# A vision-tower layer on one core: the attention weighing in fp16 parts from the second batch on, one exp for two heads, and relu's high half cast by GpSimd

## What is computed

```python
h = einsum('bhid,oi,od->bho', x, weighted_sum, weight)            # x: (8, 512, 256, 4) -> h: (8, 512, 256)
t = layernorm(h)
q, k, v = split(t @ qkv_w.T + qkv_b)                               # 16 heads of 16
q, k = unit(rotate(q)), unit(rotate(k))                            # rotary, then divided by the norm
attn = softmax(einsum('bhqd,bhkd->bhqk', q, k) * 16 ** -0.5)
h = h + einsum('bhqk,bhkd->bhqd', attn, v) @ out_w.T + out_b
y = layernorm(h)
w = sigmoid(y @ Wg + bg); w = w * (w > 0.5)                        # gates of 8 experts
h = h + sum_e w[:, e] * (relu(y @ W1[e] + b1[e]) @ W2[e] + b2[e])  # 256 -> 1024 -> 256
```

## Time and profile before

| What | us |
|---|---|
| median of 3 runs | 2003.24 |
| the profiled execution | 2003.1 |
| its span, first to last instruction | 2001.2 |
| busy TensorE matmuls in it | 1898.5 (95%) |
| busy ScalarE | 1143.7 (57%) |
| busy VectorE | 780.0 (39%) |
| busy GpSimd | 675.3 (34%) |

### The profile page before, as it was taken

One profiled execution on the slowest core, in us unless ns is written; L12 is line 12 of the kernel. 1 busy time (PEld: TensorE's weight loads), 2 busy tenths in 40 slices (PEclk: granted clock), 3 DMA queues, 4 the chain that ended last, 5 costly groups with the idle time before them and its releaser, 6 DMA issues.

```text
span 2001.2 us, 33188 instructions
## 1 busy us (share of the span) xinstructions
PE 1898.5 (95%) x13120; PEld 1207.9 (60%) x13120; DVE 780.0 (39%) x1664; ACT 1143.7 (57%) x1969; POOL 675.3 (34%) x570
## 2 busy tenths in 40 slices
PE   5679898899999999999999999999999999999999
PEld 4237543567546764577646775467645776466666
DVE  5756943547213480045602472134800456022000
ACT  2654576544765457644765547654576447655444
POOL 1103422324323353333423343233533334234443
PEclk8679999899999999999999999999999999999999
DMA  4013342242212221132212322122211322113221
GB/s 156 25 60 106 106 147 85 96 168 69 80 64 106 95 85 64 64 121 80 85 64 85 116 69 80 64 106 95 85 64 64 121 81 85 64 64 116 105 86 54
DMA packets 40475, 176.67 MB, mean 88 GB/s; under 512 B 4072, under 2 KB 17152, under 8 KB 23936
## 3 DMA queue, kind: packets, MB, share of 16 engines
q1 hardware_dynamic: 40320, 174.54, 24.9%
HBM read 153.55 MB, written 20.97 MB: 87 GB/s over the span
## 4 chain that ended last, share of the span: by engine, by line
PE 78%; DVE 8%; issue 6%; ACT 2%; POOL 1%; POOLq 0%; DVEq 0%; ACTq 0%
PE bank_h L859 29%; PE bank_f L878 10%; PE bank_f L880 10%; PE bank_f L881 10%; PE bank_o L787 5%; PE bank_s L775 3%; PE bank_s L691 3%; PE bank_s L692 2%; PE bank_s L693 2%; PE bank_s L760 1%; DVE qk L981 1%; DVE tmp_b L976 1%; DVE y L899 1%; POOL hl L547 1%; PE bank_s L827 1%
## 5 line engine op out<-in xcount | busy, mean ns | idle before, releaser
L547 POOL TENSOR_TENSOR hl<-h,hh 128x512 f16<-128x512 f32 x512 | 607.5, 1187 | 1125.5 <-ACT hh L668 693.3
L859 PE MATMUL bank_h<-x,w1s 128*128 128x512 f16 x3072 | 757.6, 384 | 9.1 <-ACT hh L668 8.6
L665 ACT ACTIVATE h<-bank_h,b1s 128x512 f32<-128x512 f32 x512 | 353.5, 690 | 450.4 <-PE bank_h L859 440.4
L878 PE MATMUL bank_f<-w2s,hh 128*128 128x256 f16 x2048 | 562.8, 275 | 1.9 <-DVE acc L1086 1.2
L880 PE MATMUL bank_f<-w2s,hh 128*128 128x256 f16 x2048 | 561.2, 274 | 0.0
L881 PE MATMUL bank_f<-w2s,hl 128*128 128x256 f16 x2048 | 561.1, 274 | 0.0
L859 PEld LDWEIGHTS bank_h<-x,w1s 128*128 128x128 f16 x3072 | 288.9, 99 | 339.1 <-ACT hh L668 45.5
L668 ACT ACTIVATE hh<-bank_h,b1s 128x512 f16<-128x512 f32 x512 | 352.5, 688 | 0.0
L634 ACT ACTIVATE probs<-bank_s 128x512 f32<-128x512 f32 x480 | 262.3, 604 | 145.6 <-PE bank_s L775 145.2
L878 PEld LDWEIGHTS bank_f<-w2s,hh 128*128 128x128 f16 x2048 | 202.1, 99 | 109.7 <-issue 42.8
L1086 DVE SCALAR_TENSOR_TENSOR acc<-bank_f,gw,acc 128x256 f32<-128x256 f32 x256 | 106.1, 477 | 364.9 <-PE bank_f L881 364.8
(11 more groups left out here) (141 smaller groups left out, 1723.7 us busy)
## 6 DMA issues: line engine op xcount, KB each, us to landing
w1s<-w_parts SPq DMA_DIRECT2D x56, 1024.0 KB, 4.8
w2s<-w_parts SPq DMA_DIRECT2D x56, 1024.0 KB, 4.8
xraw<-in_x_t_dram SPq DMA_DIRECT2D x32, 512.0 KB, 4.6
raw<-in_w_dram SPq DMA_DIRECT2D x16, 1024.0 KB, 6.8
w_parts<-w1s SPq DMA_DIRECT2D x8, 1024.0 KB, 8.8
w_parts<-w2s SPq DMA_DIRECT2D x8, 1024.0 KB, 10.6
out_dram<-acc SPq DMA_DIRECT2D x16, 256.0 KB, 6.0
raw<-in_qkv_w_t_dram SPq DMA_DIRECT2D x1, 768.0 KB, 7.4
```

The costliest lines, as they stand in the source:

```text
L547: pool.tensor_tensor(hl[n % HBUFS][:], h32[n % 2][:], hh[n % HBUFS][:], ALU.subtract)\
L665: act.activation(h32[n % 2][:], bank_h[n % 2][:, :], ACT.Relu, bias=b1s[:, e, m:m + 1]).then_inc(h_hi.sem, 1)
L859: last = pe.matmul(bank_h[n % 2][:, :], w[:, wp, k, m * P:(m + 1) * P], x16s[fb % 2][:, xp, k, :], start=(k == 0 and wp + xp == 0), stop=( ...
L878: pe.matmul(o, high, w[:, 0, m, :], start=(m == 0 and t % 2 == 0), stop=False, skip_group_check=True)
```

## The change

From the second batch on (`ab` of 1 and more), the weighing works on fp16 halves. `v16` holds the values' high and low halves; `probs` is re-read as two fp16 planes (`halves`). Each unit is weighed in three passes of four fp16 matmuls (high by high, low values by high probs, high values by low probs). The first batch keeps fp32 (`v32`, which lies in the second expert's weight tile until that is filled).

One exp per step: ScalarE reads both score banks in one instruction of 1024 columns. From the second batch on it writes into `exps`, two halves of the `qk` tile, and a new step `halves n`, 0.8 of a step after `scores n`, makes the fp16 planes: the low half is always a subtraction of 1024 columns on VectorE (L1074 of the changed kernel); the high half is cast by ScalarE for even n (right behind the exp) and by VectorE for odd n (L1071). The exp of step n waits for the halves of step n-2, and `weigh` waits for `halved`. TensorE's `scores n` waits for the whole exp of step n-1 (n-2 in the first batch, which has two pairs of banks).

Relu's high half: ScalarE does one relu per chunk; GpSimd casts `h32` to `hh` (L568), waits for its own cast, and subtracts (L570).

So that fp16 holds the values, the weights and biases of v are scaled by a power of two and those of the output projection by its inverse: a maximum over the values' weights in the first batch (`v_max`, one VectorE reduction and one GpSimd all-reduce), and `scale_values` at the head of the first pass (nine small VectorE instructions, four of 512 columns and one of 256). Each `qkv` step splits the values with two more VectorE instructions.

```diff
+        steps += [(first + PACE * n, "scores", n), (first + PACE * (n + 0.8), "halves", n)]
...
+        v16 = sb("v16", [P, 2, TT, HEADS, 2, HD], F16)
+        halves = [p[:].rearrange("p j t -> p (j t)").bitcast(F16).rearrange("p (s j t) -> p s j t", s=2, j=4)
+                  for p in probs]
+        exps = [qk[:, 2 * i:2 * i + 2, :] for i in range(2)]
...
-                    wait(pool, h_hi, fb, 2 * (n + 1))
+                    wait(pool, h_out, fb, n + 1)
                     wait(pool, f2_done, fb, n - HBUFS + 1)
+                    pool.tensor_copy(hh[n % HBUFS][:], h32[n % 2][:]).then_inc(h_hi.sem, 1)
+                    wait(pool, h_hi, fb, n + 1)
                     pool.tensor_tensor(hl[n % HBUFS][:], h32[n % 2][:], hh[n % HBUFS][:], ALU.subtract)\
                         .then_inc(h_lo.sem, 1)
...
-                    for j in range(2):
-                        wait(act, scored, ab, 2 * n + j + 1)
-                        act.activation(probs[u % 2][:, 2 * half + j, :], score_bank(2 * n + j, fb is None)[:, :], ACT.Exp,
-                                       scale=SCORE_SCALE).then_inc(exped.sem, 1)
+                    wait(act, scored, ab, 2 * n + 2)
+                    if ab == 0:
+                        terms = probs[u % 2][:, 2 * half:2 * half + 2, :]
+                    else:
+                        wait(act, qk_unit, ab, TT)
+                        wait(act, halved, ab - 1, n - 1)
+                        terms = exps[n % 2]
+                    act.activation(terms, score_banks(n, fb is None)[:, :, :], ACT.Exp, scale=SCORE_SCALE)\
+                       .then_inc(exped.sem, 1)
+                    if ab and half == 0:
+                        wait(act, exped, ab, n + 1)
+                        copy(halves[u % 2][:, 0, 0:2, :], terms).then_inc(high_even.sem, 1)
...
-                                   bias=b1s[:, e, m:m + 1]).then_inc(h_hi.sem, 1)
-                    wait(act, f2_done, fb, n - HBUFS + 1)
-                    act.activation(hh[n % HBUFS][:], bank_h[n % 2][:, :], ACT.Relu,
-                                   bias=b1s[:, e, m:m + 1]).then_inc(h_hi.sem, 1)
+                                   bias=b1s[:, e, m:m + 1]).then_inc(h_out.sem, 1)
...
+                    wait(pe, exped, ab, n - (1 if fb is None else 0))
...
-                    wait(pe, exped, ab, 4 * (n + 1))
+                    if ab == 0:
+                        wait(pe, exped, ab, 2 * (n + 1))
+                    else:
+                        wait(pe, halved, ab - 1, 2 * (n + 1))
...
+                        passes = [(v_high, p_high), (v_low, p_high), (v_high, p_low)]
+                    for k, (v, p) in enumerate(passes):
+                        for j in range(4):
+                            last = pe.matmul(bank_o[32 * j:32 * j + 32, :],
...
+                elif stage == "halves":
+                    u, half = divmod(n, 2)
+                    high, low = (halves[u % 2][:, part, 2 * half:2 * half + 2, :] for part in range(2))
+                    wait(dve, weighed, ab, u - 1)
+                    if half:
+                        wait(dve, exped, ab, n + 1)
+                        half_v.link(dve, dve.tensor_copy(high, exps[n % 2]))
+                    else:
+                        wait(dve, high_even, ab - 1, u + 1)
+                    dve.tensor_tensor(low, exps[n % 2], high, ALU.subtract).then_inc(halved.sem, 1)
```

More of the change, by code:

```diff
@@ L74, in attention_order @@
     for n in range(2 * UNITS):
-        steps.append((first + PACE * n, "scores", n))
+        steps += [(first + PACE * n, "scores", n), (first + PACE * (n + 0.8), "halves", n)]
     for u in range(UNITS):
@@ L100, in bodies @@
     attention = attention_order()
-    prep = [(0.4 + 0.9 * p, "parts", PIECES + p) for p in range(PIECES)]
+    prep = [(0.4 + 0.9 * p, "parts", PIECES + p) for p in range(PIECES)] + [(0.2, "v_scaled", 0)]
     for e in range(2, EXPERTS):
@@ L129, in merge @@
         return order
-    between = {("split", 0): [("mix_weights", 1)], ("split", 1): [("projections", 0)],
+    between = {("split", 0): [("mix_weights", 1)], ("scores", 1): [("v_max", 0)], ("split", 1): [("projections", 0)],
                ("scores", 3): [("maxima", 0), ("maxima", 1), ("reduce", 0), ("scales", 0)],
@@ L139, in bodies @@
     first = [("mix_weights", 0)]
-    for step in attention_order(alone=True):
+    for step in [s for s in attention_order(alone=True) if s[1] != "halves"]:
         first += [step[1:]] + between.get(step[1:], [])
@@ L288, in build @@
         scl = sb("scl", [P, 2])
[L290 removed]
+        vmx = sb("vmx", [P, DK])
+        vmxr = sb("vmxr", [P, DK])
+        vbound = sb("vbound", [P, 2])
+        vscl = sb("vscl", [P, 2])
+        both_s = two_banks("bank_s")
+        bank_s = [both_s[:, i, :] for i in range(2)]
         bank_m = bank("bank_m")
         bank_o = bank("bank_o")
[L293 removed]
+        both_h = two_banks("bank_h")
+        bank_h = [both_h[:, i, :] for i in range(2)]
         bank_f = [bank(f"bank_f{i}") for i in range(2)]
@@ L375, in build, with score_banks @@
         block = ctx.enter_context(nc.Block())
-        def score_bank(n, alone):
-            return ([bank_s[0], bank_s[1], bank_h[0], bank_h[1]] if alone else bank_s)[n % (4 if alone else 2)]
+        def score_banks(n, alone):
+            return both_h if alone and n % 2 else both_s
         def qkv_banks(t, alone):
@@ L672, in steps @@
                     act.wait_ge(scales, e + 1)
+                    if e == 1 and p == PIECES // 2:
+                        wait(act, weighed, 0, UNITS)
                     if e >= 2 and p == 0:
@@ L784, in steps @@
                         wait(pe, o_out, ab, g)
-                    for j in range(4):
-                        h = 4 * g + j
-                        last = pe.matmul(bank_o[32 * j:32 * j + 32, :],
-                                         v1[:, tile, h, :, :].rearrange("p s d -> p (s d)"),
-                                         probs[n % 2][:, j, :], start=(tile == 0), stop=(tile == TT - 1),
-                                         skip_group_check=True)
+                    if ab == 0:
+                        passes = [(v32[:, tile], probs[n % 2])]
+                    else:
+                        v_high, v_low = v16[:, 0, tile], v16[:, 1, tile]
+                        p_high, p_low = halves[n % 2][:, 0], halves[n % 2][:, 1]
+                        passes = [(v_high, p_high), (v_low, p_high), (v_high, p_low)]
+                    for k, (v, p) in enumerate(passes):
+                        for j in range(4):
+                            last = pe.matmul(bank_o[32 * j:32 * j + 32, :],
+                                             v[:, 4 * g + j].rearrange("p s d -> p (s d)"), p[:, j, :],
+                                             start=(tile == 0 and k == 0),
+                                             stop=(tile == TT - 1 and k == len(passes) - 1), skip_group_check=True)
                     last.then_inc(weighed.sem, 1)
@@ L1088, in steps @@
                            .then_inc(acc_done.sem, 1)
+                elif stage == "v_scaled":
+                    scale_values()
                 elif stage == "maxima":
```

77 lines of the change are left out of this document (64 added, 13 removed).

## The result

The changed kernel takes 2065.1 us (median of four runs, 2064.7 to 2066.0), the kernel before 2002.5 on the same chip: a ratio of 1.0309 [1.0297, 1.0321], 62 us slower. The forecast was 2048 us, its range 1981 to 2100, so the sign and the range hold and the size was 17 us short. The profiled execution's span is 2062.9 us.

A forecast was written before the change was run, and what follows sets the result against it. The prediction took TensorE as the bound in steady passes (busy 231.6 of 233.5 us). Its terms, +24 for six steady passes, +17 and +3 for the first pass, +1 for the first batch, gave +45 on 2003.1: 2048 us, range 1981 to 2100.

The forecast's parts named there:

- TensorE's saving: Weighing in steady passes: three fp16 rounds take 0.82 us per unit instead of 1.00, -2.9 us per pass.
- rounds that are not at full rate: Rival for the weighing: fp16 rounds take 1.3 us per unit instead of 0.82, adding 54 us, total 2100; chance 0.05.
- Relu: Steady pass: ScalarE's second relu goes, and one f1 no longer waits 1.0 us for it, -1.0 us.
- The two stalls in the stage: Scores stage: weighings behind the fifth expert's `acc` and behind the last exp each stall 1.6 us with GpSimd in the way.
- five "more places": Weighings behind the other two `acc` and three `out_turn`: some 0.4 us each with GpSimd in the way, 2.2 per pass.
- 2.5 for the shared path: Scores stage: VectorE and GpSimd exclude each other, charged 2.5 us per steady pass, bounds 0 and 6.
- Value split "0": Two more VectorE instructions per tile, about 0.9 us, lie between qkv steps 5 us apart and cost 0.
- the cast costing nothing outside the stage: GpSimd's cast of relu's high half, taken as 0.6 us: 0 in the last batch; sharing with VectorE charged in the scores stage.
- The first pass: VectorE lacks room for the halves in the scores stage: +17 us, range -3 to +35; scaling at its head another +3.
- scaling at the head: `scale_values` at the first pass's head takes some 3.6 us on VectorE before the second batch's first split: +3 (0 to 5).
- It hides: Rival: slack between steps absorbs VectorE's work, total about 1981 us; decided by weighings waiting at most 0.18 us on the mean; chance 0.25.
- The clock falls too: Rival: stalls lower TensorE's clock to 0.95 over the scores stage, 4 to 5 us per steady pass, total 2085; chance 0.15.

The follow-up runs named there:

- run 2: The kernel before with only relu's high half cast by GpSimd added: 2019.2 us, 1.0081 of the kernel before.
- run 8: The changed kernel with fp16 weighing from the third batch on, later weighings, GpSimd's cast only in chunks 24 to 47, values split behind the rotation: 1993.3 us.
- run 1: The changed kernel with relu's high half back on ScalarE: 2066.2 us, 1.0325 of the kernel before.
- run 7: The changed kernel with GpSimd casting relu's high half only in chunks 24 to 47, ScalarE elsewhere: 2055.5 us, 1.0273 of the kernel before.
- Run 11: The changed kernel with GpSimd's subtraction cut to 64 of 512 columns, leaving out 7/8 of relu's low half: 1986.2 us, 0.9918 of the kernel before.
- run 9: Run 8 with the values' scale worked out at chunk 59.3 of the first pass, not at its head: 1989.9 us, 0.9939 of the kernel before.
- run 5: The changed kernel without the low half of the values (written once as fp16, low plane zero): 2056.8 us, 1.0281 of the kernel before.
- Run 6: The changed kernel with weighings 0.9 of a step later, `out_copy` moved along and ScalarE's wait moved from exp to cast: 2029.0 us, 1.0135 of before.
- run 10: Run 8 with fp16 weighing from the second batch on, as in the changed kernel: 2008.8 us, 1.0035 of the kernel before.

## Why the prediction was right, and where it was off

**TensorE's saving: right in kind, small in size.** This is a weighing in the open, of the changed kernel:

```profile
817.85 0.83 PE L832 MATMUL bank_o<-probs,v 128*32 128x512 f16 x12
818.61 1.47 PE L904 MATMUL bank_h<-x,w1s 128*128 128x512 f16 x6
```

0.76 us per unit for the forecast 0.82; I had put gaps between fp16 rounds, and they start 0.22 apart, as matmuls of 512 columns do in an f1 (0.216). So the gain is 0.24, not 0.18: -3.8 per steady pass, where the term said -2.9. The rival of rounds that are not at full rate is refuted by the same row. The Trainium skill (TensorEngine Tiling (Array Packing), section on restrictions) has column tiling turn off the fast weight load; these twelve loads, of 96 ns on the mean, fit under the rounds, so nothing here hangs on it.

**Relu: the total right by luck, the place wrong.** The term's 1.0 was the wait of one f1 for ScalarE. That wait is still there, 1.22 us at 766.09: ScalarE's relu stands behind a step of the rotation (L644), for which it waited until VectorE was done at 764.80. The 0.8 that a steady pass did gain came in its first eighth, of which the forecast says nothing; run 2 shows it alone.

**The two stalls in the stage: right.** TensorE lost 1.5 us (pitch over the normal one) at the thirteenth weighing and 2.0 at the last; the forecast had 1.6 at each. The five "more places", 2.2 us in the sum, cost 0.6 at two weighings, and one pair of score matmuls comes 0.7 late behind an exp (799.20). With the 1.7 of the clock behind the last weighing these make 6.5. The stage as a whole is +2.4, with the saving of 3.8 a loss of 6.2 (some 0.4 of small waits of the kernel before are gone), where the terms had 2.5 + 5.4 = 7.9. Of the 6.2 the clock's 1.7 were no part of those terms; without them it is 4.5. The 2.5 for the shared path has no place of its own in the trace, though its base was too low: 16 units of two subtractions at 1.22 and one cast at 0.68, as they last with GpSimd idle, are 50 us, not 45.

**Value split "0", and the cast costing nothing outside the stage: wrong.** These are the steps that failed. I had looked for room between qkv steps, 5 us apart, and found 0.9 us easily housed. The split takes 1.84 us where it stands: its cast starts while GpSimd multiplies for the rotation (L577) and takes 1.13, where it takes 0.29 with GpSimd idle (run 8), and its subtraction 0.71 for 0.42. And what matters is which of VectorE's steps stand behind, and in this stretch VectorE was nearly full before:

```profile
722.43:747.96 25.53, 24.20 (x194) 16.47 (x192) 21.72 (x41) 16.81 (x27) 12.24 (x9) 1.00 0.19 63
```

It was busy for 21.7 of 25.5 us. In the third eighth the split alone costs 2.2 (runs 1 and 7), the cast alone 3.3 and more (run 2), both together 3.8: they don't add, since either makes VectorE late, and TensorE then waits for `acc`, or for the turning of q and k, or for both. Run 11 gives all of it back with split and cast in place, and shows the rotation's steps short again, so the exclusion with GpSimd is the mechanism, as the forecast argued, for one stage too few.

The steady pass, then: -3.8 - 0.8 + 3.8 + 6.2 = +5.4, less 0.2 in the rest, is +5.2 (+4.9 on the mean of the six), for the forecast's +4.0. That the error is so small (29 for 24 us over six passes) is luck: a term of 3.8 was missing, the saving was taken 0.9 too small and the loss in the stage 1.7 too large.

**The first pass: mis-sized, +34 for +20.** The scaling at the head was named and is right: 3.7 for +3, and moving it gave 4.4 (run 9). The value split, again, was left out: +5.9 in the second eighth, 4.0 of which go with its low half (run 5) and 3.1 with GpSimd's cast (run 1); they overlap. The stage gained 23 and the last eighth 2.6 for the term's 17, which was the upper end of the forecast's own 6 to 20 us, less 3, with all 14 us of waits for GpSimd in it. Its base counted four all-reduces (25.7 us) for a stretch of 120 us that holds three (18.3). The halves were taken at 53 us of VectorE and took 63.3 in that stage, where VectorE is busy for 114.6 us for 46.6 before, and TensorE waits 30.6 us for them in the pass. Run 11 shows that a shorter subtraction on GpSimd is worth 32 us in this pass, 13.6 of it in the stage. Run 6 shows that order gives 9.

**Rivals.** "It hides" is refuted for this order: the 16 weighings of a steady pass wait 3.7 us together, 0.23 on the mean, where 0.18 was the limit. Run 6 shows how near it was: with weighings one step later it holds in the stage. "The clock falls too" came in small: 0.99 over a steady pass, 1.3 us behind the late `acc` (twelve f2 matmuls at 0.21 for 0.11) in five of the six passes and 1.7 behind the last weighing in four. It was given as a rival of its own; behind the last weighing it is rather a surcharge on a long stall, and behind `acc` it costs nothing net, since the pass without it waits 2.49 us for VectorE instead.

The Trainium skill (SBUF — State Buffer, the section "SBUF: two separate sides") calls the pair of ports that VectorE and GpSimd share an exclusive lock, held for the whole instruction. The trace agrees, for these instructions: VectorE's subtraction takes 1.21 to 1.23 us when it starts with GpSimd idle and 1.49 to 2.18 when it starts under one of GpSimd's (run 11), so the one that starts first is not held up.

What stays open: how much of run 6 is the place of the weighings and how much ScalarE's moved wait; whether the first pass's 16 us of run 10 could be had by moving halves to ScalarE there (not tried), and how much of run 11's gain outside the third eighth is the shorter hold and how much GpSimd's earlier end.

## What to carry to other kernels

When work moves to an engine that looks idle, read its busy share stretch by stretch together with that of the engine that excludes it: 39% of the span was 85% of the third eighth, and there a split that needs 0.7 us by itself took 1.84 and cost 2.2. Before you give up such a change, move the consumer: 0.9 of a step more distance between producer and weighing, with the waits that go with it, was worth 36 us. And leave the new work out of a pass in which the receiving engine is already full.

## What the hardware showed that was not expected

- TensorE's clock after a stall, within a pass whose mean is 0.99: after a wait of 2.61 us its matmuls start at twice the pitch (0.21 for 0.11 us) for some 3 us, and after one of 3.23 (run 2) the granted clock is 0.50, the 1.2 GHz level. The length of the stall does not settle it: the clock falls after the 2.61 in five of six steady passes, after the 3.23 in three of six, after the 1.97 at the last weighing in four of six, and after the 1.42 at the thirteenth in none. A stall of 2 us at the last weighing costs 2 or 3.7.
- A lower clock can cost nothing: the third eighth takes 29.4 us with the fall and 30.5 without, where VectorE is the one that is late.
- VectorE's subtraction of 1024 columns is held up when it starts under one of GpSimd's instructions, and not when GpSimd's starts after it: 1.49 to 2.18 us (113 subtractions) for 1.21 to 1.23 (111). A cast of 256 columns went from 0.29 to 1.13 in this way.
- Fp16 rounds of four matmuls on 32 columns each start 0.22 us apart, the pitch of single matmuls of 512 columns, where the fp32 rounds of the earlier trace rows start 0.45 apart, some 0.02 over twice that pitch.
- GpSimd casts 512 columns of fp32 to fp16 in 0.61 us when alone. The Trainium skill (GPSIMD Engine Reference, section 3.1) has 0.77 as the best case of a plain loop over 512 elements; the measurement decides.
- GpSimd is held up in the same way: its cast that started under VectorE's cast (878.88) took 1.07 us for 0.61, and its subtraction that started under VectorE's subtraction (880.03) 2.02 for 1.16.
